# First four units of a shared MLP on one Trainium2 core: loads by halves, another order of requests, and a fourth unit by seven products

## The reference

```python
def mlp(x, g, u, d):                       # g, u: 256 x 1024, d: 1024 x 256
    return (gelu(x @ g) * (x @ u)) @ d
out = sum(w[b, e] * mlp(x, skill_gate[e], skill_up[e], skill_down[e]) for the 2 experts e of row b)
x = x + out + mlp(x, shared_gate, shared_up, shared_down)
lora = sum over e of cond[b, e] * (x @ As[e].T) @ Bs[e].T
x = x + x @ W_base.T + b_base + 2 * lora
```

## Time and profile before

| | |
|---|---|
| median of 3 runs | 800.66 us (800.28 to 801.05) |
| profiled execution | 800.03 us |
| its span, first to last instruction | 798.2 us |
| busy: PE, DVE, ACT, POOL | 99%, 85%, 59%, 36% of the span |
| chain that ended last | PE 99%, DMA 1% |
| granted TensorE clock, mean | 0.999 |

### The profile page before, as it was taken

One profiled execution on the slowest core, in us unless ns is written; L12 is line 12 of the kernel. 1 busy time (PEld: TensorE's weight loads), 2 busy tenths in 40 slices (PEclk: granted clock), 3 DMA queues, 4 the chain that ended last, 5 costly groups with the idle time before them and its releaser, 6 DMA issues.

```text
span 798.2 us, 13016 instructions
## 1 busy us (share of the span) xinstructions
PE 792.9 (99%) x4014; PEld 678.4 (85%) x4014; DVE 676.6 (85%) x874; ACT 470.1 (59%) x715; POOL 290.5 (36%) x266
## 2 busy tenths in 40 slices
PE   9999999999999999999999999999999999999998
PEld 7888888888888888889888889888888888898887
DVE  4886987987876898899789789988978988998986
ACT  6564564564654656576566566566656655656653
POOL 1440321321110662552255055344415615533420
PEclk9999999999999999999999999999999999999999
DMA  7340520302313442353353254335334323533300
GB/s 211 75 120 12 148 80 12 121 1 89 110 40 80 139 135 84 106 154 112 102 152 90 87 163 121 106 105 131 105 120 146 105 80 122 152 107 103 84 1 28
DMA packets 120143, 80.56 MB, mean 101 GB/s; under 512 B 62481, under 2 KB 115473, under 8 KB 120081
## 3 DMA queue, kind: packets, MB, share of 16 engines
q1 hardware_dynamic: 120080, 79.88, 34.2%
HBM read 67.28 MB, written 12.58 MB: 100 GB/s over the span
## 4 chain that ended last, share of the span: by engine, by line
PE 99%; DMA 1%; DVE 0%; ACT 0%; SPq 0%; DVEq 0%; issue 0%
PE ps_ring L736 62%; PE ps_acc L736 36%; DMA raw<-_L_cond_shared_gate_dram 1%; PE ps_acc L944 0%; PE ps_acc L964 0%; PE ps_ring L754 0%; DVE stage L1798 0%; PE ps_ring L758 0%; PE ps_ring L762 0%; PE ps_acc L850 0%; PE ps_ring L964 0%; ACT xc L1065 0%; PE ps_acc L990 0%; ACT wide L1065 0%; SPq L456 0%
## 5 line engine op out<-in xcount | busy, mean ns | idle before, releaser
L736 PE MATMUL ps_ring<-xc,wide 128*128 128x512 f32 (+1 forms) x2076 | 454.1, 367 | 0.0
L736 PEld LDWEIGHTS ps_ring<-xc,wide 128*128 128x128 f32 x2076 | 366.3, 188 | 65.5 <-issue 0.3
L1065 ACT CAST inner_hi<-post 128x512 fp32r<-128x512 f32 x192 | 117.9, 621 | 140.8 <-DVE post L1723 67.6
L1404 DVE TENSOR_TENSOR inner_lo<-post,inner_hi 128x512 fp32r<-128x512 f32 x192 | 162.1, 858 | 12.2 <-ACT inner_hi L1065 11.8
L736 PE MATMUL ps_acc<-inner_hi,wide 128*128 128x512 f32 x504 | 172.0, 390 | 0.0
L1068 ACT ACTIVATE post<-ps_ring 128x512 f32<-128x512 f32 (+1 forms) x132 | 73.3, 558 | 89.4 <-PE ps_ring L736 85.4
L736 PEld LDWEIGHTS ps_acc<-inner_hi,wide 128*128 128x128 f32 x504 | 94.7, 188 | 19.2
L695 POOL TENSOR_TENSOR post<-post 128x256 f32<-128x256 f32 x48 | 34.5, 741 | 187.7 <-DVE post L1671 187.7
L736 PE MATMUL ps_acc<-inner_lo,wide 128*128 128x512 f32 x252 | 98.3, 390 | 0.0
L1723 DVE SCALAR_TENSOR_TENSOR post<-post,coef_now,ps_ring 128x512 f32<-128x512 f32 x80 | 59.4, 742 | 30.7 <-PE ps_ring L736 25.4
L736 PE MATMUL ps_acc<-inner_hi,sh_dn 128*128 128x512 f32 x256 | 83.8, 389 | 0.0
(11 more groups left out here) (122 smaller groups left out, 863.0 us busy)
## 6 DMA issues: line engine op xcount, KB each, us to landing
raw<-n_L_cond_skill_gate_dram SPq DMA_DIRECT2D x32, 256.0 KB, 2.9
raw<-in_L_cond_skill_up_dram SPq DMA_DIRECT2D x32, 256.0 KB, 3.4
raw<-n_L_cond_skill_down_dram SPq DMA_DIRECT2D x32, 256.0 KB, 3.7
xbuf<-n_L_cond_skill_gate_dram SPq DMA_DIRECT2D x32, 256.0 KB, 2.9
xbuf<-in_L_cond_skill_up_dram SPq DMA_DIRECT2D x32, 256.0 KB, 3.3
xbuf<-n_L_cond_skill_down_dram SPq DMA_DIRECT2D x32, 256.0 KB, 3.7
xt_scratch<-xbuf SPq DMA_DIRECT2D x8, 512.0 KB, 3.2
sh_scratch<-stage SPq DMA_DIRECT2D x8, 512.0 KB, 2.8
```

Of the source, the lines that this page charges most:

```text
L736: last = pe.matmul(dst, left_[a], right_[b], start=start and n == 0, stop=stop and n == len(PASSES) - 1, skip_group_check=adds)
L1065: return nc.scalar.copy(dst, src)
L1404: return V.tensor_tensor(dst, src, hi.bitcast(F32), ALU.subtract)
```

## The change

- The gate of unit 0 comes in two DMAs, one for each half of the features; 13 in place of 20 unused transposes. `first_gate(r)` is used for row 1 as for row 0, and row 1's transposes stand between the two up outputs.
- Row 3 is asked for ahead of row 1's store and of unit 2's weights.
- All four blocks of rows 0 and 1 are copied to SBUF before the cast of unit 1's weights. POOL then makes T1 to T4 of the first quarter (`t0_a` to `t0_c`, in `post`), ACT and DVE split them (`split_first`).
- Unit 3 (`SU` = 3) is made by seven products; T1 of the first quarter lies in the place of T4 of the second, which is therefore split later. S1 to S4 of pair 3 are made by POOL and split in unit 2 ahead of its products.
- Routing is cut in three, in units 7, 11 and 15 on DVE; the exponential on ACT goes to unit 14.

```diff
@@ constants
+    SU = PAIRS - 1
+    NM = NU - SU
+        t0_a, t0_b, t0_c = (post[:, n * S:(n + 1) * S] for n in range(3))
+        s_tmp3 = post[:, 0:2 * S].rearrange("p (g n c) -> p g n c", g=2, n=4)
-        LEFT_SUMS = [5, 7, 9, 10]
+        LEFT_SUMS = [5, 7, 10, 9]
+        POOL_SUMS = [1, 2, 3, 4]
+        FIRST_SUMS = [lambda hl: right(1, hl, T4), lambda hl: right(0, hl, T3), lambda hl: right(0, hl, T2),
+                      lambda hl: right(0, hl, T4)]
+        FIRST_TMP = [t0_a, t0_b, t0_c, t0_a]
@@ SP
-            load_gate_up(0, gate0_landed, up0_landed)
+            for c in range(HC):
+                sp.dma_start(raw_part(0, GATE)[:, c, :], sg[:, c, 0:PW]).then_inc(gate0_landed[c], 16)
+            sp.dma_start(raw_part(0, UP), su[:, :, 0:PW]).then_inc(up0_landed, 16)
             ...
             store_xt(0, 0)
+            sp.wait_ge(turned, 4)
+            load_x_blocks(3, x_blk1)
             store_xt(0, 1)
             ...
             load_down(2)
-            sp.wait_ge(turned, 4)
-            load_x_blocks(3, x_blk1)
@@ POOL
             left_sums(0)
+            pool.wait_ge(xt0_in, 4)
+            G.tensor_tensor(t0_a, xt(1, 0), xt(0, 0), ALU.subtract).then_inc(t0_made, 1)
+            G.tensor_tensor(t0_b, xt(1, 1), xt(1, 0), ALU.subtract).then_inc(t0_made, 1)
+            pool.wait_ge(t0_made, 1)
+            G.tensor_tensor(t0_c, xt(1, 1), t0_a, ALU.subtract).then_inc(t0_made, 1)
+            pool.wait_ge(t0_ready, 1)
+            pool.wait_ge(t0_made, 3)
+            G.tensor_tensor(t0_a, xt(0, 1), t0_c, ALU.subtract).then_inc(t0_made, 1)
             ...
+                if u == SU - 1:
+                    pool.wait_ge(sh_landed[SU], 32)
+                    pool.wait_ge(t0_ready, 4)
+                    left_sums(SU)
@@ PE
+            def first_unit():
+                first_gate(0)
+                pe.wait_ge(left_ready, LEFT_BLOCKS[0])
+                output(0, UP, 0, 3)
                 pe.wait_ge(x_landed[1], 16)
                 for c in range(HC):
                     turn(acc[1][c], x_nat1, c)
-                output(0, UP, 0, 3)
                 output(0, UP, 2, 1)
-                output(0, GATE, 1, 0)
-                output(0, GATE, 3, 2)
+                first_gate(1)
             ...
-            for _ in range(20):
+            for _ in range(13):
             ...
-                if u < PAIRS:
+                if u < SU:
                     outputs(u, GATE)
@@ ACT, unit 0
+            take_xt(1, acc[0][1])
+            take_xt(2, acc[1][0])
+            take_xt(3, acc[1][1])
             split_left(1)
-            take_xt(1, acc[0][1])
             gelu_block(0, 1, 0)
             split_shared_down(0)
+            split_first(0, FIRST_SUMS[0](0), FIRST_TMP[0])
             gelu_block(0, 3, 2)
-            take_xt(2, acc[1][0])
-            take_xt(3, acc[1][1])
+            split_first(1, FIRST_SUMS[1](0), FIRST_TMP[1])
             inner_part(0, 0)
             inner_part(0, 1)
+            split_first(2, FIRST_SUMS[2](0), FIRST_TMP[2])
             split_sums(0)
+            split_first(3, FIRST_SUMS[3](0), FIRST_TMP[3])
@@ DVE, unit 0
             split_shared_down(0)
+            split_first(0)
             mul_block(0, 1, 3)
+            split_first(1)
             mul_block(0, 3, 1)
             inner_part(0, 0)
             inner_part(0, 1)
+            split_first(2)
             split_sums(0)
+            split_first(3)
@@ DVE, later units
-                if u == 2:
-                    route()
-                if u == 3:
-                    route_weights()
+                if u == 2 * PAIRS - 1:
+                    route_scores()
+                if u == 3 * PAIRS - 1:
+                    route_experts()
+                if u == NU - 1:
+                    route_weights()
-                if u == PAIRS:
-                    split_sums(PAIRS - 1)
             ...
+                if u == SU - 1:
+                    split_sums(SU)
-                if q > 0:
+                if u >= SU:
                     sums(u, UP)
+                    if u == SU:
+                        split_right(1, T4, t_a, rights(1, 7))
```

More of the change, by code:

```diff
@@ L245, in cond_resid_kernel @@
         ex_c12 = inner[1]
-        gate0_landed = sem("gate0_landed")
+        gate0_landed = [sem(f"gate0_landed{c}") for c in range(HC)]
         up0_landed = sem("up0_landed")
@@ L365, in matrix_no @@
         def matrix_no(u, part):
-            return 2 * (u - PAIRS) + part
+            return 2 * (u - SU) + part
         def products(u, part, n):
-            return 8 * PAIRS + NP * matrix_no(u, part) + n + 1
+            return 8 * SU + NP * matrix_no(u, part) + n + 1
         def rights(q, n):
@@ L600, in left_sums @@
                 a21, a22 = v[:, :, 0, 0:P], v[:, :, 1, 0:P]
-                s1, s2, s3, s4 = (s_tmp[:, :, n, :] for n in (S1, S2, S3, S4))
+                s1, s2, s3, s4 = ((s_tmp if j < SU else s_tmp3)[:, :, n, :] for n in (S1, S2, S3, S4))
                 G.tensor_tensor(s1, a21, a22, ALU.add).then_inc(s1_made, 1)
@@ L746, in output, with first_gate @@
                 last.then_inc(product_done, 1)
-            def first_unit():
+            def first_gate(r):
                 for c in range(HC):
-                    pe.wait_ge(left_hi, c + 1)
-                    pe.wait_ge(right_hi, c + 1)
+                    if r == 0:
+                        pe.wait_ge(left_hi, c + 1)
+                    pe.wait_ge(right_hi, 2 * r + c + 1)
                     for i, bank in ((0, 0), (1, 2)):
-                        pe.matmul(ring[bank][:], left(0, 0, GATE, BLOCKS_A[i][c]), right(0, 0, BLOCKS_B[c][0]),
+                        if r > 0 and c == 0:
+                            pe.wait_ge(sh_gelu, i + 1)
+                        pe.matmul(ring[bank][:], left(0, 0, GATE, BLOCKS_A[i][c]), right(0, 0, BLOCKS_B[c][r]),
                                   start=c == 0, stop=False)
-                    pe.wait_ge(left_ready, c + 1)
+                    if r == 0:
+                        pe.wait_ge(left_ready, c + 1)
                     for i, bank in ((0, 0), (1, 2)):
-                        pe.matmul(ring[bank][:], left(0, 1, GATE, BLOCKS_A[i][c]), right(0, 0, BLOCKS_B[c][0]),
+                        pe.matmul(ring[bank][:], left(0, 1, GATE, BLOCKS_A[i][c]), right(0, 0, BLOCKS_B[c][r]),
                                   start=False, stop=False)
-                    pe.wait_ge(right_ready, c + 1)
+                    pe.wait_ge(right_ready, 2 * r + c + 1)
                     for i, bank in ((0, 0), (1, 2)):
                         last = pe.matmul(ring[bank][:], left(0, 0, GATE, BLOCKS_A[i][c]),
-                                         right(0, 1, BLOCKS_B[c][0]), start=False, stop=c == HC - 1)
+                                         right(0, 1, BLOCKS_B[c][r]), start=False, stop=c == HC - 1)
                         if c == HC - 1:
                             last.then_inc(product_done, 1)
+            def first_unit():
+                first_gate(0)
+                pe.wait_ge(left_ready, LEFT_BLOCKS[0])
+                output(0, UP, 0, 3)
                 pe.wait_ge(x_landed[1], 16)
@@ L797, in matrix @@
                 m = matrix_no(u, part)
-                if part == GATE and q == 1:
+                if part == GATE and u < SU + PAIRS:
                     pe.wait_ge(left_ready, LEFT_SUMS[j])
@@ L823, in matrix @@
                         pe.wait_ge(v_done, m + 1)
-                    product(ring[bank][:], [left(j, hl, part, a) for hl in range(2)],
-                            [right(q, hl, b) for hl in range(2)], opens, True, not opens)\
+                    if u == SU and part == GATE and n == 1:
+                        pe.wait_ge(t0_ready, 4)
+                    rights_ = [right(1, hl, T4) if q == 0 and b == T1 else right(q, hl, b) for hl in range(2)]
+                    product(ring[bank][:], [left(j, hl, part, a) for hl in range(2)], rights_, opens, True, not opens)\
                         .then_inc(product_done, 1)
@@ L1218, in _ @@
                     split_right(qn, T3, t_b)
-                if more and j == 3:
+                if more and j == 3 and q > 0:
                     act.wait_ge(t_made, 4 * q + 4)
```

115 lines of the change are left out of this document (72 added, 43 removed).

## The result

The changed kernel takes **802.67 us** (median of 12 runs, 802.09 to 803.05), the kernel before 800.68 beside it (12 runs). The ratio is 1.0023, with a 95% interval of 1.0015 to 1.0031: slower by 2.0 us. That is a little more than the 0.2% that I had set as the bound, whose value the interval includes. The profiled execution took 802.82 (span 801.0), against 800.03 (798.2) before: +2.8.

What follows compares the result with a forecast made beforehand. PE, busy in 99% of the span, was taken to bound the kernel; +1.28 + 1.5 - 1.36 = +1.4 us on the median 800.66 gave 802.1, own range 800.8 to 803.0, 8-in-10 range 798.3 to 803.5.

Steps and rivals of the forecast that it cites:

- Start, -0.69: Unit 0: with the gate in two DMAs and 13 warm-ups, the first product starts at 6.14 instead of 6.83 us.
- Seven products, -1.36: Unit 3: 42 matmuls in place of 48, at 0.2267 us each, save 1.36 us.
- Row 3: Asked for before row 1's store, its blocks land early: DVE's 2.84 us wait goes, and DVE's own work is late next.
- G(2), +1.28: Gate stretch of unit 2 starts 1.28 us later: PE waits 2.15 us for unit 1's first product, delayed on DVE.
- a lock from a mere slowing: First quarter's sums: DVE and POOL each wait for the other's running instruction (3.0 us), against merely running slower (3.2 lost).
- G(3), +1.5: Gate stretch of unit 3 loses 1.5 us: unit 2's DVE products wait behind POOL's sums, fourth ending at 56.35.
- No PE idle from 60 us on: Sign to look for in the trace: PE never stands still after the first units.
- Rest ... I take 0: Unit 3's other DVE work and the routing moved to units 7, 11 and 15 cost 0, covered by idle time.
- B: Rival: only the stall at unit 2's gate comes, unit 2's POOL chain ends in time; 800.6 us, chance 0.18.
- C: Rival: new halves fit in DVE's gaps and PE never waits; -2.24, so 798.4 us, chance 0.20.
- D: Rival: unit 0's half gate lands no earlier, everything 0.69 us later; 802.8 us, chance 0.12.
- E: Rival: one more stall, in units 3 or 4 or where routing went; forecast + 1.3, 803.4 us, chance 0.12.

Runs made afterwards that it cites:

- y3: Kernel before with only the gate in two DMAs, 13 warm-up transposes and row 1's transposes between the up outputs: 801.67 us, ratio 1.0008.
- y2: Kernel before with 17 waits on DVE and 7 on ACT that never wait (9 and 4 more instructions): 800.80 us, ratio 1.0001.
- x3: Changed kernel with POOL making unit 3's weight sums ahead of unit 2's, and the second quarter's T3 low half moved to unit 3: 801.07 us, ratio 1.0004.
- z1: Changed kernel with 47 waits on DVE and 57 on ACT that never wait, put in the first unit: 801.28 us, ratio 1.0008.
- z3: Changed kernel with 47 waits that never wait on DVE alone: 801.86 us, ratio 1.0018.
- x1: Changed kernel with POOL's four row sums of the first quarter replaced by fills with zero (results not the reference's): 799.86 us, ratio 0.9988.
- z2: Kernel before with 34 waits on DVE and 14 on ACT that never wait (17 and 7 more instructions): 802.17 us, ratio 1.002.
- y5: Kernel before with only row 3 asked for ahead of row 1's store and unit 2's weights: 800.08 us, ratio 0.9994.
- x4: Changed kernel with both the DVE order of x2 and the POOL order of x3: 799.53 us, ratio 0.9984.
- y1: x4 with 47 waits on DVE and 57 on ACT that never wait, put in the first unit: 798.36 us, ratio 0.997.
- x2: Changed kernel with DVE making unit 1's first two products earlier, around its transposes, and the second quarter's B11 half in unit 2: 801.55 us, ratio 1.001.

## Why the prediction came out as it did

The time was 0.57 above the predicted 802.1, inside the range, on the side to which I gave 0.37. But the sum held for a partly wrong reason, and that the number came so near is luck: two errors of opposite sign, one of them a loss that I had put at nothing. Step by step:

1. **Start, -0.69.** In the profiled execution 6.54 and -0.29: the first half of the gate had landed at 5.49, not 4.9. In seven of the ten profiled kernels with this start the first product begins at 6.18, near my 6.14, and in y3 the half is there by 5.03. G(1) starts at 26.12 to 26.86 in these ten and at 26.92 to 27.76 in the four with the old start, 0.8 earlier on average. So the term held on average, and the profiled execution was a late one. The half landed between 4.76 and 5.48 in these ten; the whole gate landed at 5.75 to 5.80 in three of the four with the old start, but at 4.80 in the fourth (y2), so a landing also scatters by as much as the halving was to gain. What a start is worth depends on what G(2) hangs on. With the new sums it hangs on PE's start and follows it: G(2) comes 9.96 or 9.97 after G(1) in the changed kernel, x3, z1 and z3. In y3 it hangs on row 3, which SP asked for 0.88 later than before, and the start gains nothing.
2. **Seven products, -1.36.** The stretch at 62.01 has 21 matmuls in 4.76, as 24 took 5.44.
3. **Row 3.** Its blocks were issued from 13.87 to 20.4, up to 0.9 later than I had it, and DVE no longer waits. What was late next was DVE's own work. Right.
4. **G(2), +1.28.** Measured +1.42, of it 1.8 of stall (forecast 2.15); transposes of row 3 at 29.34 (29.15), product ending at 36.45 (36.3). Here too two errors nearly cancel: PE started 0.4 later than forecast, and DVE's chain behind it was some 0.25 shorter. In x3 and z3, where the first product is at 6.18, G(2) starts at 36.24 and 36.21, only 1.07 and 1.04 later than before. x1 shows that POOL's reading sums are the cause. Its time doesn't tell a lock from a mere slowing, since the sum would be the same; the rows of the changed kernel do. POOL's second and third sums end at 17.59 and 19.29 and the halves of DVE that began beside them at 18.14 and 19.84, each 0.55 later, about the time of a half alone; and the fourth sum, which began first (19.92), takes its full-speed 1.29 while the half that began at 20.36 ends at 21.76.
5. **G(3), +1.5.** Measured 1.3 (0.17 ahead of it, then 1.1 ahead of its matmuls at 55.09 and 56.28); products at 52.37 (52.5), the fourth ending at 56.23 (56.35). The 0.2 that I took off "for the operands' being taken ahead" is the difference: PE went on at 56.28, 0.05 behind the product's end and not ahead of it. x3 shows the cause.
6. **"No PE idle from 60 us on": wrong.** Where the routing went nothing stalled, but PE lost 1.27 at the jumps. This is the step that failed: "Rest ... I take 0". I had costed the edit by its instructions' durations, and not by what their number does to the code behind them; that was 1.39 us on the median. z2 and z1 show it from both sides.

**The sum against the median.** Parts 1 to 5 came to +1.4, and the profiles say +1.42. But I laid it on the median, which was 0.63 above the profiled execution, as if that 0.63 would stay. The change without J is worth not +1.4 but +0.57 on the median (z1, whose interval is -0.2 to +1.4), and J adds 1.39 (802.67 - 801.28). Two errors, -0.8 and +1.4, left 0.57. What the 0.63 was is not shown. y5 speaks for the wait for row 3: asked for early, it goes, and the median falls by as much, though the interval includes no change. Of the three traces with the old queue and the old start, PE is kept at G(2) for 0.19 (before), 1.2 (y2) and not at all (z2). A later start is the other candidate: G(1) starts at 26.92 in the profiled execution of before and at 27.04, 27.35 and 27.76 in y2, z2 and y5.

A slip in the range: part 5's lower bound (0 for 1.5) and the 0.3 of part 4 give 802.1 - 1.8 = 800.3, where I wrote 800.8. Nothing hangs on it.

The rivals: B, one stall only, fell; C, the change does what it says, fell for this order, and x4 with the padding (y1) reaches it: 798.36 against C's 798.4. D (the half gate no earlier) happened for half its size in the profiled execution, 6.54 for 6.14, and not in most others. E named one more stall of 1.3 in the wrong place.

**What the engines wait for at the jump.** The page counts the packets of the engines' instruction queue; in the changed kernel, in z3 and in z1:

```profile
q14 instruction: 41, 0.34, 0.2%
```

```profile
q14 instruction: 31, 0.25, 0.1%
```

```profile
q14 instruction: 22, 0.17, 0.1%
```

The DMA view of single stretches says when. From 447 to 750 us, which takes in both jumps, there are 20 packets of this queue (8 KB each) in the kernel before, y2, z2 and the changed kernel, 10 in z3, and none in y1 and z1, which have no stand. Before and in the changed kernel, from ACT's first jump to ACT's next work (450.78 to 453.42, and 452.25 to 456.98):

```profile
q14 instruction: 2, 0.02, 1.9%
```

```profile
q14 instruction: 4, 0.03, 2.2%
```

| | packets before ACT's next work | before DVE's next work |
|---|---|---|
| before, y2 | 2 | 3 |
| z2, changed | 4 | 5 |
| z3 | 2 | 3 |
| y1, z1 | 0 | 0 |

The counts are the same at the second jump, and the other kernels with J (x1 to x4) have 4 and 5 as well, y3 to y5 2 and 3. When the loop ends and the branch isn't taken (at 721 to 725 us), no packet follows, and the next work comes 2.5 us (DVE) and 1.8 (ACT) behind the branch in every kernel, both waits for PE. So the stand goes with the loading of code, and it is longer where more packets come before its end; how many packets are loaded in all (42 in the kernel before, 42 in z2) doesn't set it. In z3, where half the packets are gone, ACT goes on only after two and as late as in z2 (4.9). That fits one packet for each engine ahead of the short stand's end and two ahead of the long one's, but the trace doesn't say whose a packet is. The Trainium skill, "Runtime: NRT & Kernel Launch", section "Instruction fetch mechanics", says that a taken branch whose target isn't among the code that is loaded must have it fetched before the engine goes on. That agrees with these packets; which blocks are in place at the jump no run here shows.

Open: why a shift of 17 and 7 instructions asks for more packets first and one of 9 and 4 does not. I did not try further shifts, to find where the long stand begins and ends.

## What to carry to other kernels

- If one engine's long instructions lock another's, new work "in the gaps" costs twice; put what the tensor engine waits for ahead of what nobody needs yet. Here that order alone turned +2.0 us into -1.2.
- In a kernel with a loop, adding instructions ahead of it can move the time: here by 1.4 us. Compare the engines' first work after the jump, and the instruction queue's packets there, in both traces before explaining a small difference, and repeat the better kernel with a few idle instructions in front.
- A sum of differences belongs on the profiled execution. Ask what makes the median differ from it, and whether the change removes that.

## What the runs showed of the hardware

- After a taken jump back in a loop of 323 instructions on DVE and 303 on ACT, the next work came 3.2 to 3.5 us (DVE) and 2.6 to 2.9 (ACT) later with three and two packets of 8 KB of code loaded before it, 5.4 to 5.8 and 4.5 to 4.9 with five and four, and 2.7 and 1.9, both then waits for PE, where none was loaded (y1, z1).
- A fill on POOL did not hold up DVE's low half of 128x1024 (1.22, as alone), where a sum did (1.48), and beside sums the halves of 128x512 took 1.3 to 1.8 for 0.69.
- The first two products start 0.31 apart in the changed kernel's profile and 0.56 to 0.57 apart in those of x1, y1 and z1, with the same PE code, at a granted clock of 1.00 in all of them. The difference moves G(1) by some 0.4 us: with the first product at 6.18 to 6.19, it starts at 26.25 and 26.28 where they are 0.31 apart (z3, x3) and at 26.63 to 26.72 where they are 0.56 apart (y1, z1, x2). The column of the clock doesn't show it.
